# Attention of a macaron block on one core: two bank rings turned round for every other batch, the V projection two steps later, and the last batch's statistics moved

## The reference

```python
x = x + 0.5 * ffn(layernorm(x))
x = x + attn(layernorm(x), Wq, bq, Wk, bk, Wv, bv, Wo, bo)   # 16 heads of 8, softmax over 256 keys
x = x + 0.5 * ffn(layernorm(x))

def ffn(x):                      # ternary weights, a scale for each output
    h = silu(tlin(x, w1)) * tlin(x, w2)        # 128 -> 512
    h = gelu(tlin(h, h1))                      # 512 -> 512, exact gelu
    h = gelu(tlin(h, h2))                      # 512 -> 512
    return tlin(h, w3)                         # 512 -> 128
```

## Time and profile before

| what | us |
|---|---|
| median of 3 runs (lowest, highest) | 666.66 (664.96, 670.3) |
| the profiled execution's own time | 672.58 |
| its span | 670.8 |
| busy in the span: TensorE matmuls | 630.9 (94%) |
| TensorE weight loads | 462.1 (69%) |
| VectorE | 440.4 (66%) |
| ScalarE | 466.8 (70%) |
| POOL | 92.4 (14%) |
| one even batch in the middle of attention (batch 8, from 351.3) | 15.1 |
| one odd batch (batch 9, from 366.4) | 15.9 |

### The profile page before, as it was taken

One profiled execution on the slowest core, in us unless ns is written; L12 is line 12 of the kernel. 1 busy time (PEld: TensorE's weight loads), 2 busy tenths in 40 slices (PEclk: granted clock), 3 DMA queues, 4 the chain that ended last, 5 costly groups with the idle time before them and its releaser, 6 DMA issues.

```text
span 670.8 us, 12974 instructions
## 1 busy us (share of the span) xinstructions
PE 630.9 (94%) x4452; PEld 462.1 (69%) x4452; DVE 440.4 (66%) x1036; ACT 466.8 (70%) x791; POOL 92.4 (14%) x256
## 2 busy tenths in 40 slices
PE   1969999999999799999999999999999999999996
PEld 1748878788776566666666566666567878878785
DVE  4844666858545867877878887784076485656742
ACT  2646786968864357777777868774477796887964
POOL 2601010012101012222222222102001001010000
PEclk9969999999999679999999999995689999999999
DMA  9100000000051704370715343300000001001011
GB/s 296 41 2 1 1 0 0 1 0 0 1 195 56 251 2 153 101 245 13 249 62 189 118 133 127 128 1 1 1 3 1 1 0 33 0 0 31 1 31 33
DMA packets 36674, 41.97 MB, mean 63 GB/s; under 512 B 2448, under 2 KB 27280, under 8 KB 36624
## 3 DMA queue, kind: packets, MB, share of 16 engines
q1 hardware_dynamic: 36624, 41.31, 18.2%
HBM read 22.42 MB, written 18.87 MB: 62 GB/s over the span
## 4 chain that ended last, share of the span: by engine, by line
PE 82%; DVE 7%; ACT 4%; issue 3%; DMA 2%; POOL 0%; SPq 0%; ACTq 0%; POOLq 0%
PE bank L1008 45%; PE bank L1118 10%; PE bank L1092 7%; PE bank L1105 5%; PE bank L1107 4%; DVE neg_max L816 2%; PE bank L1150 2%; PE bank L1136 2%; ACT probs L630 1%; PE bank L1081 1%; PE bank L1073 1%; PE bank L1055 1%; DVE act_lo L766 1%; PE bank L1077 1%; DMA QK<-qk_scratch 1%
## 5 line engine op out<-in xcount | busy, mean ns | idle before, releaser
L1008 PE MATMUL bank<-act_hi,WH 128*128 128x512 f32 x576 | 233.3, 405 | 6.8 <-issue 5.4
L1008 PE MATMUL bank<-act_lo,WH 128*128 128x512 f32 x576 | 228.8, 397 | 0.0
L816 DVE TENSOR_REDUCE neg_max<-bank 128x2 f32<-128x512 f32 x256 | 166.9, 682 | 50.0 <-PE bank L1092 46.8
L630 ACT ACTIVATE probs<-bank 128x512 f32<-128x512 f32 x256 | 140.8, 597 | 54.6 <-PE bank L1107 52.5
L786 DVE TENSOR_TENSOR act_lo<-full,act_hi 128x512 fp32r<-128x512 f32 x128 | 88.0, 689 | 124.2 <-ACT act_hi L529 124.1
L527 ACT ACTIVATE full<-bank,SG 128x512 f32<-128x512 f32 x128 | 88.0, 687 | 69.1 <-PE bank L1008 68.7
L1008 PEld LDWEIGHTS bank<-act_hi,WH 128*128 128x128 f32 x576 | 109.1, 189 | 37.2 <-issue 6.0
L1008 PEld LDWEIGHTS bank<-act_lo,WH 128*128 128x128 f32 x576 | 109.1, 189 | 25.4 <-issue 0.5
L1105 PE MATMUL bank<-QK 32*128 32x256 f32 x512 | 113.0, 348 | 3.5 <-ACT probs L630 1.8
L1107 PE MATMUL bank<-m_parts,SEL 32*128 32x256 f32 x512 | 96.0, 293 | 0.0
L1092 PE MATMUL bank<-QK 32*128 32x256 f32 x512 | 83.1, 340 | 6.7 <-DVE neg_max L816 4.8
(11 more groups left out here) (91 smaller groups left out, 597.2 us busy)
## 6 DMA issues: line engine op xcount, KB each, us to landing
qk_scratch<-qk SPq DMA_DIRECT2D x64, 256.0 KB, 2.6
QK<-qk_scratch SPq DMA_DIRECT2D x16, 1024.0 KB, 7.2
X<-x SPq DMA_DIRECT2D x4, 512.0 KB, 6.9
raw_rest<-w_ffn SPq DMA_DIRECT2D x4, 512.0 KB, 6.1
out<-X SPq DMA_DIRECT2D x4, 512.0 KB, 3.2
raw<-w_ffn SPq DMA_DIRECT2D x3, 256.0 KB, 4.4
WA<-w_att SPq DMA_DIRECT2D x1, 256.0 KB, 5.2
xT<-sel SPq DMA_DIRECT2D x1, 256.0 KB, 5.1
```

The source lines that it names most:

```text
L630: A.activation(probs[:, v % 8, :], bank[B_BANKS[v]][:, :], ACT.Exp, scale=SCALE)\
L816: D.tensor_reduce(neg_max[:, bb, qt, n0:n0 + 2], bank[banks[u]][:, :].rearrange("p (h k) -> p h k", h=2), axis=AX.X, op=ALU.max, negate=Tr ...
L1008: ins = MM(dst, a, b, start=k == 0, stop=k == len(todo) - 1)
```

## The change

There are three edits.

**Banks.** `A_BANKS` and `B_BANKS` become pairs of tuples, one for even and one for odd batches: even ones go 0, 1, 5, 0, 1, 5 ... and end on 0; odd ones go 5, 1, 0 ... and end on 5 (scores: 2, 3, 7 and 7, 3, 2). The distance is three for units 3 to 15 in both. Unit 0 of a batch now has two, unit 1 four and unit 2 three. `used_last` finds the distance across the border between batches, also from `ENTRY_BANKS` into batch 1.

**V at step 9.** `project_v` on TensorE and `set_v` on ScalarE stand at step 9 of an even batch instead of step 7.

**Statistics.** The 8-tile statistics of the second feed-forward part move on VectorE from the steps 7 to 11 of batch 14 to the steps 2 to 6 of batch 15, and the normalising that uses them from step 3 to step 10 of batch 15; on POOL the reciprocal root stands after `max_again` of batch 15 instead of before it.

```diff
--- before.py
+++ after.py
@@ -51,8 +51,8 @@
 TOKENS = 13
 GATE_BANKS = (0, 1, 4, 0, 1, 4, 0, 1)
 UP_BANKS = (2, 3, 5, 2, 3, 5, 2, 3)
-A_BANKS = (0, 1, 5) * 4 + (0, 1, 5, 1)
-B_BANKS = (2, 3, 7) * 4 + (2, 3, 7, 3)
+A_BANKS = ((0, 1, 5) * 5 + (0,), (5, 1, 0) * 5 + (5,))
+B_BANKS = ((2, 3, 7) * 5 + (2,), (7, 3, 2) * 5 + (7,))
 ENTRY_BANKS = (0, 3, 1, 2) * 4
 PARTS_OF = ((0, 0, 1, 1), (0, 1, 0, 1))
 LOADS, WRITES = 16, 16 * 8
@@ -283,6 +283,12 @@
                 at.append((1, u - SKEW + UNITS))
             return [(d, v) for d, v in at if 0 <= v < UNITS + 4]
 
+        def used_last(banks, prev, u):
+
+
+            before = prev + banks[:u]
+            return next((d for d in range(1, len(before) + 1) if before[-d] == banks[u]), u + 1)
+
         def q_of(ring):
 
             return QK[:, RING - 1 - ring, 0, :, :]
@@ -478,8 +484,8 @@
             add_bias(NBATCH - 5)
             max_again(NBATCH - 2, 0)
             add_bias(NBATCH - 4)
+            max_again(NBATCH - 1, 1)
             rsqrt_steps(NORMS1, K * NORMS1)
-            max_again(NBATCH - 1, 1)
             with pool.Fori(NBATCH - 3, NBATCH) as b:
                 add_bias(b)
             norms(NORMS1 + 1, NORMS1 + NP, 8)
@@ -623,11 +629,11 @@
 
             ffn_phase(0)
 
-            def exp_unit(b, v):
+            def exp_unit(b, bb, v):
                 act.wait_ge(b_mm, UNITS * b + v + 1)
 
                 act.wait_ge(pv_mm, GROUPS * b + v // 4 - 2 + 1 + CREDIT)
-                A.activation(probs[:, v % 8, :], bank[B_BANKS[v]][:, :], ACT.Exp, scale=SCALE)\
+                A.activation(probs[:, v % 8, :], bank[B_BANKS[bb][v]][:, :], ACT.Exp, scale=SCALE)\
                     .then_inc(exp_done, 1)
 
             def evacuate_o(b):
@@ -643,20 +649,20 @@
                 act.wait_ge(on_T, b + 1)
                 A.activation(onT[:, :], bank[6][:, 0:SEQ], ACT.Copy).then_inc(on_T_sb, 1)
 
-            def attend(b, prev=True, prev2=True, own=True, steps=UNITS, ahead=None, v_pair=None):
+            def attend(b, bb, prev=True, prev2=True, own=True, steps=UNITS, ahead=None, v_pair=None):
 
 
                 for u in range(steps):
                     for d, v in in_step(u, prev, own):
                         if v < UNITS:
-                            exp_unit(b - d, v)
+                            exp_unit(b - d, (bb + d) % 2, v)
                         if v == UNITS + 3:
                             evacuate_o(b - d)
                     if u == 1 and own:
                         top_max(b)
                     if u == 3 and prev2:
                         o_to_sbuf(b - 2)
-                    if u == 7 and v_pair is not None:
+                    if u == 9 and v_pair is not None:
                         set_v(*v_pair)
                     if u == 7 and ahead is not None:
                         x_to_sbuf(ahead)
@@ -670,8 +676,8 @@
                         split_x(NB + 1, 1, 5)
 
             def att_body(i, par, ahead=True, more=True, first=False):
-                attend(2 * i, prev=not first, prev2=not first, v_pair=(i + 1, 1 - par) if more else None)
-                attend(2 * i + 1, prev2=not first, ahead=i + 2 if ahead else None)
+                attend(2 * i, 0, prev=not first, prev2=not first, v_pair=(i + 1, 1 - par) if more else None)
+                attend(2 * i + 1, 1, prev2=not first, ahead=i + 2 if ahead else None)
 
             att_body(0, 0, first=True)
             att_body(1, 1)
@@ -680,7 +686,7 @@
                 att_body(2 * n + 1, 1)
             att_body(NPAIR - 2, 0, ahead=False)
             att_body(NPAIR - 1, 1, ahead=False, more=False)
-            attend(NBATCH, own=False, steps=SKEW + 4)
+            attend(NBATCH, 0, own=False, steps=SKEW + 4)
             ffn_phase(1)
 
 
@@ -809,12 +815,12 @@
                 dve.wait_ge(bv_out, 1)
                 D.tensor_tensor(BO[:, :], bank[3][:, 0:P], BO[:, :], op=ALU.add).then_inc(bias_set, 1)
 
-            def max_unit(b, bb, u, banks=A_BANKS):
+            def max_unit(b, bb, u, banks=None):
                 dve.wait_ge(a_mm, UNITS * b + u + 1)
                 qt, jj, lane = a_unit(u)
                 n0 = 32 * lane + 2 * jj
                 D.tensor_reduce(neg_max[:, bb, qt, n0:n0 + 2],
-                                bank[banks[u]][:, :].rearrange("p (h k) -> p h k", h=2), axis=AX.X,
+                                bank[(banks or A_BANKS[bb])[u]][:, :].rearrange("p (h k) -> p h k", h=2), axis=AX.X,
                                 op=ALU.max, negate=True).then_inc(max_done, 1)
 
             def split_max(b, bb):
@@ -943,7 +949,7 @@
 
             ffn_phase(0)
 
-            def attend(b, bb, prev=True, prev2=True, more=True, steps=(), norm=None):
+            def attend(b, bb, prev=True, prev2=True, more=True, steps=(), steps_at=7, norm=None, norm_at=3):
 
 
 
@@ -954,13 +960,13 @@
                         split_max(b, bb)
                     if u == 6 and prev2:
                         add_att(b - 2, 2 * b - 4)
-                    if u == 3 and norm is not None:
+                    if u == norm_at and norm is not None:
                         n, tile0, width = norm
                         normalise(n, tile0, 0)
                         if width > 4:
                             normalise(n, tile0 + 4, 4)
-                    if u >= 7:
-                        for step in steps[u - 7:u - 6]:
+                    if u >= steps_at:
+                        for step in steps[u - steps_at:u - steps_at + 1]:
                             step()
                     if u == TOKENS + 1 and prev:
                         norm_o(b - 1)
@@ -972,12 +978,14 @@
                 if ahead:
                     q = i + 2
                     steps, norm = norm_steps(norm_of(q), 4 * q, 4), (norm_of(q), 4 * q, 4)
-                elif not more:
-                    steps, norm = norm_steps(NORMS1, 0, biased=4), (NORMS1, 0, 8)
                 else:
                     steps, norm = (), None
                 attend(2 * i, 0, prev=not first, prev2=not first, steps=steps)
-                attend(2 * i + 1, 1, prev2=not first, more=more, norm=norm)
+                if more:
+                    attend(2 * i + 1, 1, prev2=not first, norm=norm)
+                else:
+                    attend(2 * i + 1, 1, more=False, steps=norm_steps(NORMS1, 0, biased=4), steps_at=2,
+                           norm=(NORMS1, 0, 8), norm_at=10)
 
             att_body(0, 0, first=True)
             att_body(1, 1)
@@ -1082,12 +1090,11 @@
                              start=True, stop=True)
                 ins.then_inc(v_mm, 1)
 
-            def max_scores(b, par, bb, u, banks=A_BANKS):
+            def max_scores(b, par, bb, u, banks, prev):
 
                 qt, jj, lane = a_unit(u)
                 rows = slice(32 * lane, 32 * lane + 32)
-                ahead = next(d for d in range(1, UNITS) if banks[u - d] == banks[u])
-                wait(pe, max_done, UNITS * b + u - ahead + 1)
+                wait(pe, max_done, UNITS * b + u - used_last(banks, prev, u) + 1)
                 for i in range(2):
                     ins = MM(bank[banks[u]][:, SEQ * i:SEQ * i + SEQ],
                              q_of(2 * par + bb)[rows, 2 * jj + i, P * qt:P * qt + P],
@@ -1098,10 +1105,9 @@
 
                 jj, kt, lane = b_unit(v)
                 rows = slice(32 * lane, 32 * lane + 32)
-                last = next(d for d in range(1, UNITS) if B_BANKS[v - d] == B_BANKS[v])
-                wait(pe, exp_done, UNITS * b + v - last + 1 + CREDIT)
+                wait(pe, exp_done, UNITS * b + v - used_last(B_BANKS[bb], B_BANKS[1 - bb], v) + 1 + CREDIT)
                 for i in range(2):
-                    dst = bank[B_BANKS[v]][:, SEQ * i:SEQ * i + SEQ]
+                    dst = bank[B_BANKS[bb][v]][:, SEQ * i:SEQ * i + SEQ]
                     MM(dst, k_of(2 * par + bb)[rows, 2 * jj + i, P * kt:P * kt + P],
                        q_of(2 * par + bb)[rows, 2 * jj + i, :], start=True, stop=False)
                     ins = MM(dst, SEL[rows, 2 * jj + i, :], m_parts[rows, bb, :], start=False, stop=True)
@@ -1171,7 +1177,7 @@
                                 pe.wait_ge(qk_loaded[0], LOADS)
                             if u == 1:
                                 pe.wait_ge(v_set, 1)
-                            max_scores(0, 0, 0, u, ENTRY_BANKS)
+                            max_scores(0, 0, 0, u, ENTRY_BANKS, ())
                     pe.wait_ge(h_full, hl + 6)
                     before = nb + 2 * i - 2
                     hidden(g, 0, 0, h_lo, hl + HT, general, {2: tokens} if into_att else {})
@@ -1290,7 +1296,7 @@
 
                 for u in range(steps):
                     if more:
-                        max_scores(b + 1, npar, nbb, u)
+                        max_scores(b + 1, npar, nbb, u, A_BANKS[nbb], A_BANKS[bb] if prev else ENTRY_BANKS)
                     for d, v in in_step(u, prev, own):
                         at = (b - d, par, bb) if d == 0 else (b - d, ppar, pbb)
```

## The result

The changed kernel takes 643.62 us (median of 4 runs, 641.54 to 646.73), against 666.68 us beside it (664.96 to 670.3): a ratio of 0.9651, with a 95% interval of 0.9589 to 0.9713. A second set of runs on another occasion gave 643.45 us and 0.9587 (0.9504 to 0.9670). The ratios compare only those executions of a kernel that lie near its fastest. The prediction was 645, range 638 to 659. The profiled execution took 641.84 us, with a span of 640.0 instead of 670.8.

The account below looks back on a forecast made before the run. Attention was taken as bound by small repeated waits of TensorE, a stall in batch 14 and the slow clock behind it. Terms 12.3 + 0.4 + 3.9 + 9.3 - 0.3 = 25.6 us gave 647.0 or 641.1; forecast 645, range 638 to 659.

Parts of the forecast that it names:

- Terms 1 and 2: Bank waits of scores (steps 2, 3) and maxima (steps 14, 15): 0.49 us each batch; 0.5 even, 0.35 odd.
- Two of the signs: In the profile after: steps 2 and 3 take about 1.1 us, steps 14 and 15 about 0.7.
- Term 3: V at step 9 of even batches fills the maxima's time: up to 0.77 us won at step 11.
- Term 4: DVE limits gains: even batch 1.6 us, odd 0.45; pair 2.05, six pairs 12.3, batch 1 0.4, batch 0 none.
- the place, as a rival: Slower: the clock recovers later after batch 0, each further batch costing 5.0 us; chance 0.04.
- Term 5: Batch 14 without statistics: 13.1 us instead of 17.00, gain 3.9, of which about 1.4 stall and 1.5 clock.
- Term 6: Clock stays at 1.00 through batch 15: 12.0 us instead of 21.30, gain 9.3, lower bound 0.
- Term 7: Statistics and normalising in batch 15 cost 0, covered by the batch; 1 to 2 us if that cover is gone.
- Term 8: Entry: batch 1's first maxima, on bank 5, wait for all 16 maxima of batch 0; -0.3 us.
- The two bases: Sum of 25.6 us taken from profiled 672.58 gives 647.0, from median 666.66 gives 641.1; median put at 645.
- VectorE taking the gain back: Batches 2 to 13: busy DVE cuts the steady gain from 12.3 to 4.2 us, giving 649 to 655; chance 0.10.
- The fallen clock in batch 15: Clock falls anyway in batch 15, losing 9.3 and 1.5 us of gain, giving 652 to 658; chance 0.24.

Follow-up runs that it names:

- e7: Changed kernel with VectorE's 4-tile statistics moved from the even batches to the odd batches before them; 639.17 us, 0.9531 against the kernel before.
- e10: Changed kernel with V at step 7 in batch 0 alone, step 9 elsewhere; 645.81 us, 0.9682.
- e1: Changed kernel with V back at step 7 and the statistics back in batch 14, leaving the two bank rings alone; 662.29 us, no ratio.
- e2: Kernel before with the V projection and its copy at step 9 alone; 658.84 us, 0.9789 against the kernel before.
- e11: Changed kernel with the 8-tile statistics back in batch 14 in one step and POOL's old order; 655.09 us in one run.

## Why the prediction was right

- **Terms 1 and 2, banks:** right in mechanism and size. 0.49 and 0.47 us a batch for the scores (0.49 forecast), 0.46 and 0.37 for the maxima (0.5 and 0.35), each measured alone. Two of the signs were off by 0.2 us: steps 2 and 3 take 0.91 (1.1 forecast), because 0.16 of their wait now falls into step 1, whose transposes start 0.90 us into the batch instead of 0.74; and steps 14 and 15 take 0.90 (0.7 forecast).
- **Term 3, V:** right. 0.77 us in an even batch, exactly the stall behind step 8, and nothing in odd ones. V itself costs the same 1.09.
- **Term 4, VectorE's limit:** the sum was somewhat too low. A pair gained 2.29 us (1.72 and 0.57), not 2.05, and the batches 2 to 13 13.6, not 12.3. The limit that I allowed for in the even batch is not there: with 1.1 us less of VectorE's work it stays at 13.36. A backlog reaches the odd batch, as forecast, and costs 0.28 (`e7`). It is lost not in step 1, where I had put it, but in the steps 6 and 7, behind the normalising.
- **The same term, batch 0:** wrong. I put rings and V at 0 there, since the slow clock covers the waits. In the profiled pair batch 1 starts 2.7 us earlier. The windows of batch 0 (20.1 and 15.8) overstate that, since 1.6 of their difference is a later first matmul (term 8). What this gain goes with is the clock, which came back at 237.4 instead of 244.4. Nor does the slow clock cover all waits: with V alone the whole of batch 0 ran at 0.50, and from the transposes of step 1 to batch 1 it took 16.8 us instead of 17.7. With the rings there and V at step 7 (`e10`) it took 17.4, against 14.6 to 15.2 in the seven profiles with V at step 9; that is one profile, and why the clock came back earlier stays open. I had named the place, as a rival, with the sign reversed.
- **Term 5:** 4.3 for 3.9 in the profiled pair. At a full clock 1.4 of it is the stall, and 0.9 the rings (13.7 to 12.75; 0.6 forecast); the other 2.0 go with the clock, which was 0.82 over batch 14 before.
- **Term 6, the clock:** 8.6 for 9.3 in the profiled pair, and the cause holds as a likelihood (six of seven against none of seven), not as a rule. Batch 15 took 12.7, where I had 12.0.
- **Term 7:** right. The normalising of 2.65 us ended in step 14 or 15 of batch 15, the norming of batch 14 right behind it, and TensorE took that up 3.1 us later:

```profile
446.47 2.65 DVE L760 TENSOR_SCALAR xn<-X,moments,rstd 128x128 f32<-128x128 f32 x8 [3.40 <-POOL rstd L405]
449.05 0.29 DVE L842 RECIPROCAL o_sum<-bank 128x24 f32<-128x24 f32 x1
```

- **Term 8:** the first matmul of batch 1's maxima came at 224.3 instead of 222.7, as said. It cost nothing, instead of 0.3: the transposes of step 1, which need all maxima of batch 0 anyway, came at 225.06 us instead of 225.12.
- **The two bases:** the profiled execution gained 30.7 us where the sum said 25.6; the median gained 23.1 where I said 21.7. The 5.1 us that the sum lacked are the entry (2.7 instead of -0.3), the batches 1 to 14 (2.2 too little), and the steps behind batch 15 (2.0, no term); against them stand batch 15 (0.7 too much) and the second feed-forward part (-1.4, no term). I had put the median 3.9 above what the sum gave from 666.66, without a row behind the size; it was 7.6 less than the profiled gain. The direction was right, as the median's executions had less to win from the clock. That 645 lies only 1.4 from 643.62 is in part luck: two errors of 5.1 and 3.7 us with opposite signs.
- **Rivals:** VectorE taking the gain back is refuted by `e1`, `e2` and the even batch of `e7`, but for 0.15 us in an odd batch. The fallen clock in batch 15 is not seen in any of seven profiles without the stall, though that ring of three banks keeps cycling.

## What to carry to other kernels

Where an engine's busy share is modelled, subtract the starts of repeated groups: two free steps beside two held ones priced three of the edits to 0.1 us. A ring of buffers needs its distances checked over the loop's border, and work that needs no ring belongs into the ring's wait, not ahead of it. One long operation on a helper engine costs its stall, and may cost several times that through TensorE's clock: batches 14 and 15 of `e11` took 37.3 us against 25.5 in the changed kernel, for a stall of 1.4. Cut it into pieces or move it where nobody waits, and compare such kernels at the same granted clock.
